# Routed rows turned on VectorE instead of TensorE, router in column tiles: a perceiver layer with a mixture of experts

## The reference, cut to what matters

```python
shared = silu(xt @ Wg_s) * (xt @ Wu_s) @ Wd_s
logits = xt @ W_router + routing_bias            # 7 experts
probs = jax.nn.sigmoid(logits)
scores, idx = jax.lax.top_k(probs, TOPK)         # TOPK = 2
scores = scores / jnp.sum(scores, axis=-1, keepdims=True)
...
hmid = silu(g) * u                               # g, u: xt by each expert's Wg_r, Wu_r
combined = jnp.einsum('tei,eih,te->th', hmid, Wd_r, wts)
return (shared + combined).reshape(B, S, H)
```

## Time and profile before

| | us |
|---|---|
| median of 3 runs | 812.71 (811.16 to 813.4) |
| the profiled execution's own time | 809.95 |
| its span, first to last instruction | 808.1 |
| PE busy in the span | 773.6 (96%) |
| DVE busy | 517.4 (64%) |
| ACT busy | 355.5 (44%) |
| POOL busy | 301.0 (37%) |

### The profile page before, as it was taken

The page is one execution under the profiler, slowest core; times in us unless marked ns, Lnnn a source line. Parts: engine busy times, 40 slices in busy tenths (PEclk is TensorE's granted clock), DMA queues, the critical chain, the costliest instruction groups (busy, mean ns, idle before and its releaser), DMA issues.

```text
span 808.1 us, 17427 instructions
## 1 busy us (share of the span) xinstructions
PE 773.6 (96%) x6752; PEld 574.0 (71%) x6753; DVE 517.4 (64%) x1125; ACT 355.5 (44%) x913; POOL 301.0 (37%) x157
## 2 busy tenths in 40 slices
PE   4799999999899999989999999899999999999996
PEld 3555455554657778878867877788888888888884
DVE  5799798788652447777788887855364333443335
ACT  4356545661443248852178768523432122211221
POOL 1000000000442833732032213533649999993034
PEclk9999999999899999999999999999999999999999
DMA  9968756683520050040388000030485355531138
GB/s 341 390 252 327 259 218 243 262 326 122 219 105 1 0 149 13 2 138 0 105 312 314 1 0 1 22 137 25 183 306 210 112 206 167 191 135 52 52 114 275
DMA packets 46576, 127.04 MB, mean 157 GB/s; under 512 B 4001, under 2 KB 8353, under 8 KB 40369
## 3 DMA queue, kind: packets, MB, share of 16 engines
q1 hardware_dynamic: 36752, 105.44, 35.9%
q10 hardware_dynamic: 7200, 12.32, 4.4%
q0 software_dynamic: 2560, 8.39, 3.1%
HBM read 101.99 MB, written 24.15 MB: 156 GB/s over the span
## 4 chain that ended last, share of the span: by engine, by line
PE 81%; DVE 5%; DMA 5%; POOL 3%; ACT 3%; issue 2%; SPq 0%; DVEq 0%; ACTq 0%; POOLq 0%
PE scores L611 11%; PE bank L641 11%; PE bank L1137 7%; PE bank L1139 7%; PE bank L1138 7%; DMA nat<-in_ctx_keys 3%; PE bank L691 2%; POOL picked L1379 2%; PE bank L845 2%; PE bank L693 2%; PE bank L851 2%; PE bank L692 2%; PE bank L846 2%; PE bank L626 2%; PE bank L881 2%
## 5 line engine op out<-in xcount | busy, mean ns | idle before, releaser
L1844 DVE STREAM_TRANSPOSE ctxT<-nat 128x1024 f32<-128x1024 f32 (+3 forms) x124 | 116.9, 1004 | 7.8 <-DMA nat<-in_ctx_keys 7.5
L641 PE MATMUL bank<-nat,probT 128*64 128x512 f32 (+1 forms) x416 | 93.9, 597 | 0.1
L1366 POOL TENSOR_TENSOR ring_lo<-ring_raw,ring_hi 128x2048 fp32r<-128x2048 f32 x18 | 83.0, 4611 | 14.5 <-ACT ring_hi L1732 13.3
L1244 POOL TENSOR_TENSOR wq_lo<-wq_raw,wq_hi 128x1024 fp32r<-128x1024 f32 x4 | 9.3, 2352 | 207.6 <-ACT wq_hi L1477 207.6
L1137 PE MATMUL bank<-ring_hi,xg_lo 128*128 x180 | 74.2, 412 | 0.0
L1139 PE MATMUL bank<-ring_hi,xg_hi 128*128 x180 | 70.6, 392 | 0.0
L1138 PE MATMUL bank<-ring_lo,xg_hi 128*128 x180 | 70.1, 389 | 0.0
L2488 DVE TENSOR_TENSOR rhm_lo<-bank,rhm_hi 128x512 fp32r<-128x512 f32 x21 | 14.5, 692 | 80.2 <-ACT rhm_hi L1743 80.2
L641 PEld LDWEIGHTS bank<-nat,probT 128*64 128x64 f32 (+1 forms) x416 | 27.9, 136 | 51.6 <-issue 48.1
L1749 ACT COPY hn<-bank 128x512 f32<-128x512 f32 x22 | 12.9, 588 | 112.0 <-PE bank L1139 112.0
L611 PE MATMUL scores<-ctxT,hn 32*64 32x416 f32 (+8 forms) x1536 | 55.2, 426 | 5.1 <-issue 2.7
(11 more groups left out here) (317 smaller groups left out, 1936.1 us busy)
## 6 DMA issues: line engine op xcount, KB each, us to landing
nat<-in_ctx_keys SPq DMA_DIRECT2D x48, 1024.0 KB, 8.1
ring_raw<-in_Wexp SPq DMA_DIRECT2D x21, 1024.0 KB, 6.3
x_slots<-zeros SPq DMA_DIRECT2D x1, 5632.0 KB, 18.2
y_slots<-zeros SPq DMA_DIRECT2D x1, 5632.0 KB, 32.7
hn<-x_slots ACTq DMA_DIRECT2D x22, 256.0 KB, 4.5
y_slots<-hn ACTq DMA_DIRECT2D x22, 256.0 KB, 3.0
w_raw<-in_Wexp SPq DMA_DIRECT2D x3, 1024.0 KB, 5.3
nat<-in_ctx_keys SPq DMA_DIRECT2D x16, 130.0 KB
```

Source lines behind the costliest of these rows:

```text
L641: last = nc.tensor.matmul(context_bank(k)[64 * b:64 * b + 64, :], probT[0:n, j, 64 * b:64 * b + 64], nat[k % 2][0:n, b, j, :], start=j == ...
L1366: last = nc.gpsimd.tensor_tensor(ring_lo[at], ring_raw[at], ring_hi.bitcast(F32)[at], ALU.subtract)
L1844: dve.transpose(dst, src).then_inc(columns_ready, 1)
```

## The change

Three edits.

1. The rows of a tile are loaded by four DMAs into a blocked layout: partition 32c + q, place g holds row 32g + q, columns 128c to 128c + 127. One DVE transpose of 32 x 32 blocks (`dve.transpose`, STREAM_TRANSPOSE) of the whole 128 x 512 tile then gives feature columns on the partitions, in the order that `by_block` describes; the rows of the routed gate and up weights and the norm weights (`V_W2B`, four more columns of `vec`) are permuted on the host to match. PE's four transposes a tile and their waits are gone.
2. `xg_hi` and `xg_lo` are now made from `xgT`, a tile in SBUF, where they were made from a PSUM bank. POOL's list is unchanged.
3. The router's matmuls take the 128 tokens in four column tiles of 32: 16 matmuls for a group of 128 tokens, in place of 4.

```diff
-        xg = hn[0:2]
+        xg = [t.rearrange("p (g f) -> p g f", f=P) for t in hn[0:2]]
+        xgT = place(150, "xgT", [P, HC, P])
+        def slot_rows(t):
+            return x_slots[ds(t * P, P), :].rearrange("(g q) (c f) -> c q g f", q=B32, f=P)
...
             def router(k):
                 pe.wait_ge(xf_act if k < 2 else xf_ready, k + 1 if k < 2 else k - 1)
                 for c in range(HC):
-                    last = nc.tensor.matmul(bank[3][:, NE * k:NE * k + NR], xf[k % 4][:, c, :], wrout_sb[:, c, :],
-                                            start=c == 0, stop=c == HC - 1)
+                    for m in range(P // B32):
+                        own = slice(B32 * m, B32 * (m + 1))
+                        last = nc.tensor.matmul(bank[3][own, NE * k:NE * k + NR], xf[k % 4][:, c, own], wrout_sb[:, c, :],
+                                                start=c == 0, stop=c == HC - 1, skip_group_check=True)
                 last.then_inc(logit_full, 1)
...
-            def rows_columns(t, par, turn):
-                pe.wait_ge(xg_loaded[par], 16 * turn)
-                if not (isinstance(t, int) and t < 2):
-                    pe.wait_ge(xgT_ready, t - 1)
-                for c in range(HC):
-                    last = nc.tensor.transpose(bank[6 + par][:, c * P:(c + 1) * P], xg[par][:, c * P:(c + 1) * P], ident)
-                last.then_inc(xgT_full, 1)
...
             def load_rows(t, par):
-                nc.scalar.dma_start(xg[par][:], x_slots[ds(t * P, P), :]).then_inc(xg_loaded[par], 16)
+                for c in range(HC):
+                    nc.scalar.dma_start(xg[par][B32 * c:B32 * (c + 1)], slot_rows(t)[c]).then_inc(xg_loaded[par], 16)
...
-            def rows_columns_out(t, par):
+            def rows_columns(t, par, turn):
                 nth = dve.value_load(tile_expert[0:1, 1, ds(t, 1)], min_val=1, max_val=NR)
+                dve.wait_ge(xg_loaded[par], 64 * turn)
+                if not (isinstance(t, int) and t == 0):
+                    dve.wait_ge(xgT_ready, t)
+                dve.transpose(xgT[:].rearrange("p a (g q) -> p a g q", q=B32),
+                              xg[par].rearrange("p g (a e) -> p a g e", e=B32)).then_inc(xgT_full, 1)
                 dve.wait_ge(xgT_full, t + 1)
-                columns = [bank[6 + par][:, c * P:(c + 1) * P] for c in range(HC)]
-                weights = [vec[:, V_W2 + c:V_W2 + c + 1] for c in range(HC)]
                 for c in range(HC):
-                    last = dve.tensor_scalar(xg_hi[par][:, c, :], columns[c], weights[c], None, ALU.mult)
+                    last = dve.tensor_scalar(xg_hi[par][:, c, :], xgT[:, c, :], vec[:, V_W2B + c:V_W2B + c + 1], None, ALU.mult)
                 last.then_inc(xg_split, 1)
                 dve.wait_ge(xg_split, t + 1)
                 dve.wait_ge(split_ready, nth)
                 for c in range(HC):
-                    last = dve.scalar_tensor_tensor(xg_lo[par][:, c, :], columns[c], weights[c], xg_hi[par].bitcast(F32)[:, c, :],
-                                                    ALU.mult, ALU.subtract)
+                    last = dve.scalar_tensor_tensor(xg_lo[par][:, c, :], xgT[:, c, :], vec[:, V_W2B + c:V_W2B + c + 1],
+                                                    xg_hi[par].bitcast(F32)[:, c, :], ALU.mult, ALU.subtract)
                 last.then_inc(xgT_ready, 1)
```

More of the change, by code:

```diff
@@ L53 @@
 LN_EPS = 1e-5
-V_GAMMA, V_BETA, V_W1, V_W2, V_U, V_V, V_END = 0, 4, 8, 12, 16, 24, 32
+V_GAMMA, V_BETA, V_W1, V_W2, V_U, V_V, V_W2B, V_END = 0, 4, 8, 12, 16, 24, 32, 36
 NEG = -1e30
@@ L1140, in routed_product, with routed_hidden @@
                 last.then_inc(full, 1)
-            def rows_columns(t, par, turn):
-                pe.wait_ge(xg_loaded[par], 16 * turn)
-                if not (isinstance(t, int) and t < 2):
-                    pe.wait_ge(xgT_ready, t - 1)
-                for c in range(HC):
-                    last = nc.tensor.transpose(bank[6 + par][:, c * P:(c + 1) * P], xg[par][:, c * P:(c + 1) * P], ident)
-                last.then_inc(xgT_full, 1)
-            def routed_hidden(t, par, at, turn=None):
+            def routed_hidden(t, par, at):
                 if not (isinstance(t, int) and t < 2):
@@ L1163, in routed_hidden @@
                         hidden_columns(0)
-                    if m == gate and turn is not None:
-                        rows_columns(t + 1, 1 - par, turn)
             def hidden_columns(t):
@@ L1207, in _ @@
                     at = places_of(0, 3)
-                if k >= NT - 2:
-                    pe.wait_ge(hm_ready, NJ)
-                    rows_columns(k - NT + 2, k % 2, 1)
             routed_hidden(0, 0, at[0])
             for t in (1, 2):
-                routed_hidden(t, t % 2, at[t], (t + 1) // 2 + 1)
+                routed_hidden(t, t % 2, at[t])
                 routed_output(t - 1, (t - 1) % 2, at[t - 1])
@@ L1219, in _ @@
                     t = 2 * i + 4 - par
-                    routed_hidden(t, par, at[n + 1], i + 3)
+                    routed_hidden(t, par, at[n + 1])
                     routed_output(t - 1, 1 - par, at[n])
@@ L2489, in hidden_split @@
                                   hi.bitcast(F32)[:].rearrange("p c q -> p (c q)"), ALU.subtract).then_inc(rhmT_ready, 1)
-            rows_columns_out(0, 0)
+            rows_columns(0, 0, 1)
             down_out(NT - 1)
-            rows_columns_out(1, 1)
+            rows_columns(1, 1, 1)
             routed_mult(0)
@@ L2498, in _ @@
                     t = 2 * i + 1 + par
-                    rows_columns_out(t + 1, par)
+                    rows_columns(t + 1, par, i + 2)
                     routed_mult(t)
@@ L2524, in columns, with by_block @@
         return np.asarray(v).reshape(-1, P).T
+    def by_block(w):
+        return np.asarray(w).reshape(*np.shape(w)[:-2], HC, P // B32, B32, np.shape(w)[-1]).swapaxes(-4, -3).reshape(np.shape(w))
     arrays = {
@@ L2530 @@
         "vecs": np.concatenate([columns(v) for v in (L0_attn_gamma, L0_attn_beta, L0_ffn_w_ln1, L0_ffn_w_ln2,
-                                                     L0_attn_u_bias, L0_attn_v_bias)], axis=1),
+                                                     L0_attn_u_bias, L0_attn_v_bias,
+                                                     by_block(np.asarray(L0_ffn_w_ln2).reshape(D, 1)))], axis=1),
         "rows": np.concatenate([np.asarray(L0_attn_bout), np.asarray(L0_ffn_routing_bias)])[None, :],
@@ L2536 @@
         "Wexp": np.stack([np.concatenate([np.asarray(s)[None], np.asarray(r)]) for s, r in (
-            (L0_ffn_Wg_s, L0_ffn_Wg_r), (L0_ffn_Wu_s, L0_ffn_Wu_r), (L0_ffn_Wd_s, L0_ffn_Wd_r))]),
+            (L0_ffn_Wg_s, by_block(L0_ffn_Wg_r)), (L0_ffn_Wu_s, by_block(L0_ffn_Wu_r)), (L0_ffn_Wd_s, L0_ffn_Wd_r))]),
         "Wrouter": L0_ffn_W_router,
```

## The result

| | before | after |
|---|---|---|
| median of 4 runs, us | 812.56 (811.16 to 813.4) | 921.67 (920.09 to 922.73) |
| profiled execution, us | 809.95 | 922.73 |
| its span, us | 808.1 | 920.9 |
| mean granted clock of PE | 0.994 | 0.935 |

The changed kernel takes 1.134 times as long, 95% interval 1.132 to 1.137: 109 us more, where 97 (910 us) were forecast.

What follows compares the result with a forecast made beforehand. PE was taken to bound the kernel, 81% of the span, with POOL's splits close beside. Terms of 31.3 + 16.7 + 57 - 8.3 - 2.1 + 5 = +99.6 on 812.7 gave 912, stated as 910; range 860 to 938.

Steps and rivals of the forecast that it cites:

- experts 1 and 2: Tiles 1 and 2: all eight turns delay tile 1 while POOL splits to 637.8; gate(2) +31.3 us.
- expert 3: Tile 4's rows: about three instructions pass, five take a turn each behind POOL's splits; gate(4) +16.7 us.
- experts 4, 5, 6: At each expert's split, rows wait for POOL's turns; between +13 and +21.6, taken as 19 us each, +57.
- clock after the stalls: PE's lower clock after five stalls loses 2 us each, half of it behind DVE: +5 us.
- PE's transposes: Routed tiles from tile 3 on: PE saves 0.46 us in each of 18 blocks, -8.3 us.
- router: Router blocks of two groups take 0.69 us on column tiles instead of 1.71; -2.1 us, between +2 and -3.
- start of gate(0): At tile 0 DVE's transpose is exposed, so gate(0) starts at about 596.75 instead of 596.45: +0.3 us.
- The turn, 4.1 us: Each of a tile's eight DVE instructions waits one POOL instruction, 4.1 us, between bounds of 0.2 and 8.2.
- Rival A: The eight's SBUF source does not collide; POOL's list binds at tile 16: -4.7 us, 808; chance 0.09.
- B: Only the four SCALAR_TENSOR_TENSOR take turns, the four TENSOR_SCALAR pass: +78 us, 890; chance 0.14.
- C: A group of four DVE instructions passes in one turn, two waits a tile: +53 us, 865; chance 0.12.
- D: The TENSOR_SCALAR lose two turns each, limited by POOL's own list: +119 us, 931; chance 0.10.

Runs made afterwards that it cites:

- quarters: Changed kernel with each of GpSimd's split instructions cut into four 128x512 blocks, same elements; 859.57 us, ratio 1.0595 to the kernel before.
- half-kernel: Changed kernel with a second VectorE transpose into PSUM: multiplications read SBUF, differences PSUM, 875.5 us; the reverse, 880.17 us.
- PSUM version: Changed kernel with VectorE's transpose writing to the PSUM bank, where the eight multiplications and differences read it; 812.83 us, ratio 1.001 to the kernel before.
- the router alone: Kernel before with only the router's matmuls put in column tiles; 809.3 us against 811.66, ratio 0.9971.
- the last kernel above: Kernel before with the column router and ScalarE's rounding of the third expert's weights, on another chip; 812.96 us, ratio 0.9984.

## Why the prediction was right

| step of the prediction | forecast | measured |
|---|---|---|
| experts 1 and 2 | +31.3 | +28.1 |
| expert 3 | +16.7 | +20.2 |
| experts 4, 5, 6 | 3 x 19 | 20.1, 20.1, 20.1 |
| clock after the stalls | +5 | +9.3 |
| PE's transposes | -8.3 | -8.5 |
| router | -2.1 | -1.8 in the records, -2.4 (-3.7 to -1.0) by runs |
| start of gate(0) | +0.3, within the +31.3 | +2.5 |
| work ahead of the router | 0 | +2.3 |
| sum | +99.6 | +112 |

The forecast of 910 is 11.7 us short of the 921.7 measured, and the largest part of that is in sizes named below. The step that decides was right and is shown: the source of the eight alone makes the loss (812.8 and 932.8 us), and whether VectorE passes is counted in GpSimd's instructions, not in elements (859.6 with quarters). The long instructions of the earlier trace rows, of one and of eight elements, were a true sign for these. The turn, 4.1 us, was the right choice between 0.2 and 8.2: of the 176 instructions of these two lines, 31 took over 1 us, where some 33 were forecast. A blocked tile's eight took 23.6 us and not the "some 33" of the text, because a list of POOL's has only six instructions; the sum had counted with that.

The prediction left open whether a multiplication with one SBUF tensor and a pointer scalar, writing fp32r, is such an instruction: the half-kernel with only these in SBUF answers yes, with a mean of 1205 ns against 343 to 345 from PSUM. The Trainium skill (SBUF — State Buffer, Who interferes with whom) counts tensor_scalar among the operations that can enter a two-port mode, and says of the lock that it holds for the whole instruction; both agree with the runs, the second by the quarters: shorter instructions of GpSimd, shorter waits.

Rival A's condition was met by the PSUM version, and it came as priced in kind, a wait for POOL at tile 16, but with 6.0 us on DVE instead of some 8 and 812.8 instead of 808. B fell to the half-kernels: multiplications alone cost 62 us. C fell too; three of four lose a turn of their own. D did not occur.

One size came out near for another reason than forecast. For experts 1 and 2 all eight turns were put on tile 1 and none on tile 2. Measured, tile 1 lost four, because POOL's list had a gap there, and tile 2 lost three. On POOL:

```profile
606.56 9.02 POOL L1360 TENSOR_TENSOR ring_lo<-ring_raw,ring_hi 128x2048 fp32r<-128x2048 f32 x2 [0.91 <-ACT ring_hi L1726]
```

That the sum held, +28.1 for +31.3, is due to the end of the list, forecast at 637.8 and measured at 640.2, and not to the turns as they were laid out.

Three sizes were off. Experts 3 to 6: in all four lists the tile's rows met POOL near its first instruction, so nearly the full +21.6 came, 20.1, not the 19 between two bounds and not 16.7. The clock: 2 us per stall, half of it hidden, was taken from a short thin stretch; the tile behind a 20 us stall took 1.5 to 1.7 us more, the one behind the first stall 2.8, all of it on the path. And gate(0): the price of the transpose at tile 0 was counted from the end of `down_out`, 594.02, as if the rows were there. They were not:

```profile
599.38 0.49 PE L1144 MATMUL bank<-ring_hi,xg_lo 128*128 x1 [3.24 <-DVE xg_lo L2474]
```

DVE waited 2.05 us for the transfer before its first transpose, while the second expert's weights were loading beside it; with these held back, PE's idle time there fell from 3.1 to 2.0 us. The 2.3 us that the changed kernel is late before the router begins (519.88 against 517.58) belong to no step. In the profile of the router alone they are 0.6 (518.20), and in that of the last kernel above, which keeps the old rows, gate(0) starts at 597.61. They read as the spread of the work ahead of the mixture, which no experiment was made to settle.

Of the router one reading goes too far: from 64 pairs in 0.69 us the prediction concludes that overlapping tiles do not each pay a fixed cost per matmul. The row shows only that the pairs do not pay it one after another, at 10.8 ns each. If four column tiles work side by side, one tile's pairs come some 43 ns apart, and the row leaves open what each pays.

## What to carry to other kernels

Before an operand moves from PSUM to SBUF on VectorE, look what GpSimd has queued at that time: the price is up to one GpSimd instruction for each VectorE instruction that reads it (six for eight in a blocked tile here), and everything behind it in VectorE's list pays too. If the operand must move, let the transpose write to PSUM: it cost 727 ns there against 712, and the 109 us did not arise. If neither can be, cut GpSimd's instructions short or make VectorE's fewer; here that took back 62 and some 35 of the 109 us. And look then at GpSimd's list: once nothing holds the other engines up, it may end last.

## What the runs showed of the hardware

- A VectorE transpose of 128x512 from SBUF to SBUF never waited for GpSimd: 711 to 715 ns in 22 cases, 6 of them with a GpSimd split running beside, and 711 to 714 in the quartered kernel, 15 of 22 beside one. A multiplication of a quarter of its size took up to 4.57 us.
- Eight instructions pass in six turns in each of the four lists of six. In expert 4's list the second multiplication began at 707.82 and took 0.28 us: it passed in GpSimd's own gap of some 0.08 us, between a rounding (to 707.82) and its remainder (from 707.89). The eighth instruction came when the list was at its end. The other two such gaps let only one pass each. This was read from the times, not tried.
- VectorE's passing costs GpSimd little: its 18 remainders took 4.50 to 4.60 us in the changed kernel, and 4.56 to 5.00 with a median of 4.86 beside instructions of 128x512. In the kernel before they took 4.59 to 4.62.
- 64 pairs of weight load and matmul on column tiles of 32 took 0.72 us in the router, 11 ns a pair, and 0.69 from first start to the next product in the earlier stage of the earlier trace rows.
